# A routed two-layer kernel: eight weight buffers instead of six, loads asked for six tiles ahead instead of four, and other places for one phase's side steps

## The reference

```
x = x + 0.5 * ffn(layernorm(x))      # top 3 of 12 experts, hidden 512
x = x + attn(layernorm(x))           # gated linear recurrence over a sequence, norm, gated matmuls
x = x + 0.5 * ffn(layernorm(x))      # same weights as the first

# ffn: topw, sel = top_k(x @ Wg, 3); softmax over topw
# h = gelu(x @ Wup[e] + bup[e]);  y = h @ Wdown[e] + bdown[e];  sum over the 3 chosen, weighted
```

## Time and profile before

| | |
|---|---|
| median of 3 runs | 636.06 us (634.11 to 636.55) |
| the profiled execution | 638.49 us, span 636.8 us |
| TensorE matmul, weight load | busy 89%, 84% of the span |
| VectorE, ScalarE, GpSimd | busy 55%, 66%, 66% |
| HBM | 96.6 MB read, 30.8 MB written |

### The profile page before, as it was taken

How to read it: one execution, slowest core, us unless ns; L and a number is a source line. 1 busy time by engine, 2 the same in 40 slices (tenths; PEclk the granted TensorE clock), 3 DMA queues, 4 the chain that set the end, 5 groups by cost and what they waited for, 6 DMA issues and landing times.

```text
span 636.8 us, 17884 instructions
## 1 busy us (share of the span) xinstructions
PE 567.4 (89%) x4591; PEld 532.4 (84%) x4591; DVE 349.0 (55%) x1636; ACT 418.8 (66%) x1280; POOL 418.3 (66%) x432
## 2 busy tenths in 40 slices
PE   8469999999899999999989889999998999999505
PEld 7359999999799889979889878889988999999502
DVE  5973365472114688977717568887762632232206
ACT  2546686686466797888657578977766866666204
POOL 1147777777777774556677777046667777777774
PEclk9768999999899999999999899999999999999857
DMA  7676777789598776566488867365659798775137
GB/s 215 178 197 171 216 209 200 220 211 270 157 284 255 218 231 174 139 187 185 132 250 222 268 171 224 105 194 182 181 162 271 210 285 245 216 216 174 48 117 243
DMA packets 121846, 127.90 MB, mean 201 GB/s; under 512 B 17177, under 2 KB 84560, under 8 KB 121748
## 3 DMA queue, kind: packets, MB, share of 16 engines
q1 hardware_dynamic: 106452, 99.52, 52.6%
q0 software_dynamic: 12992, 26.11, 14.8%
q10 hardware_dynamic: 2304, 1.11, 0.6%
HBM read 96.62 MB, written 30.79 MB: 200 GB/s over the span
## 4 chain that ended last, share of the span: by engine, by line
PE 49%; POOL 15%; DMA 12%; issue 10%; DVE 8%; SPq 5%; ACT 1%; DVEq 0%; POOLq 0%; ACTq 0%
PE ps L930 18%; PE ps L943 17%; POOL YG L738 7%; POOL xs L722 4%; DMA xl<-xn,SG 4%; PE ps L798 3%; POOL yk L749 2%; SPq L562 2%; PE ps L900 2%; DMA xs<-XN,SX 2%; DMA yk<-Ys,row 2%; PE ps L824 2%; DMA WU<-in_L_ffn_Wup_dram 2%; POOL xl L707 2%; DMA YG<-ys,SY 2%
## 5 line engine op out<-in xcount | busy, mean ns | idle before, releaser
L1096 ACT ACTIVATE hT<-ps,BU 128x128 f32<-128x128 f32 x944 | 268.6, 371 | 120.4 <-PE ps L930 116.7
L930 PE MATMUL ps<-xT,WU 128*128 128x128 f32 x1888 | 256.2, 279 | 12.8 <-DMA WU<-in_L_ffn_Wup_dram 8.7
L943 PE MATMUL ps<-WD,hT 128*128 x1888 | 252.9, 278 | 2.7 <-DVE Ys L1634 1.8
L930 PEld LDWEIGHTS ps<-xT,WU 128*128 128x128 f32 x1888 | 234.7, 195 | 23.5 <-issue 13.4
L943 PEld LDWEIGHTS ps<-WD,hT 128*128 128x128 f32 x1888 | 232.8, 194 | 4.2 <-issue 4.2
L722 POOL DMA_INDIRECT xs<-XN,SX x144 | 144.3, 1002 | 95.1 <-issue 74.0
L738 POOL DMA_INDIRECT YG<-ys,SY x144 | 150.5, 1045 | 45.2 <-issue 41.8
L1634 DVE TENSOR_TENSOR Ys<-ps,BD 128x128 f32<-128x128 f32 x236 | 67.7, 289 | 204.0 <-PE ps L943 198.1
L707 POOL DMA_INDIRECT xl<-xn,SG x59 | 60.1, 1018 | 31.0 <-issue 13.1
L749 POOL DMA_INDIRECT yk<-Ys,row x59 | 58.8, 996 | 18.0 <-issue 11.6
L1073 ACT ACTIVATE xT<-ps 128x512 f32<-128x512 f32 (+1 forms) x55 | 32.6, 593 | 7.1 <-PE ps L900 3.3
(11 more groups left out here) (255 smaller groups left out, 539.1 us busy)
## 6 DMA issues: line engine op xcount, KB each, us to landing
WU<-in_L_ffn_Wup_dram SPq DMA_DIRECT2D x236, 256.0 KB
ys<-Ys SPq DMA_DIRECT2D x42, 256.0 KB
xl<-xs SPq DMA_DIRECT2D x118, 66.0 KB, 1.9
xl<-xs SPq DMA_DIRECT2D x59, 64.0 KB, 2.0
WD<-in_L_ffn_Wdown_dram SPq DMA_DIRECT2D x12, 256.0 KB, 5.1
WD<-yk SPq DMA_DIRECT2D x4, 768.0 KB, 7.2
xs<-XN,SX POOLq DMA_INDIRECT x144
YG<-ys,SY POOLq DMA_INDIRECT x144
```

What stands on the lines that cost most here:

```text
L930: x = e.matmul(HB[i % 2][:, c * P:(c + 1) * P], WU[i % NW][:, c * P:(c + 1) * P], xT[m % 2][:, j * P:(j + 1) * P], start=True, stop=True)
L943: x = e.matmul(YB[i % 2][:, 0:D], hT[i % 3][:, c * P:(c + 1) * P], WDf[:, bass.ds(r + c * P, P)], start=(c == 0), stop=(c == C - 1))
L1096: x = e.activation(hT[i % 3][:, c * P:(c + 1) * P], HB[i % 2][:, c * P:(c + 1) * P], ACT.Gelu, bias=BU[:, bass.ds(b + c, 1)])
```

## The change

`NW` goes from 6 to 8. At tile `i` SP asks for the weights of tile `i + 6`; at the very first tile for those of 4, 5 and 6. And the last four numbers of each entry of `CHAIN`, the places in the third phase, are others; those of the second phase, the tables and the fourth phase's lists stay.

```
-NW = 6
+NW = 8
...
-    ("V", "G0", (10, 17, 25, 30, 10, 17, 24, 30)),
-    ("V", "G2", (14, 20, 27, 34, 14, 20, 26, 32)),
-    ("V", "S1", (15, 21, 28, 36, 15, 20, 27, 33)),
-    ("A", "G", (17, 23, 29, 38, 17, 22, 28, 35)),
-    ("PA", "A1", (18, 24, 31, 39, 18, 23, 30, 36)),
-    ("PA", "A2", (18, 25, 34, 40, 18, 24, 33, 39)),
-    ("V", "C1", (18, 26, 35, 42, 18, 25, 33, 40)),
-    ("AV", "C2", (19, 27, 37, 42, 19, 25, 35, 41)),
-    ("V", "C3", (23, 28, 38, 43, 21, 26, 35, 41)),
-    ("P", "A3", (24, 30, 39, 44, 23, 28, 37, 43)),
-    ("V", "S3", (24, 30, 39, 45, 23, 28, 37, 43)),
-    ("V", "S3'", (24, 31, 39, 46, 23, 29, 37, 44)),
-    ("A", "A3", (25, 33, 40, 47, 24, 30, 39, 45)),
-    ("PA", "A4", (27, 34, 41, 49, 25, 32, 40, 46)),
-    ("PA", "A5", (28, 35, 42, 50, 26, 34, 42, 48)),
-    ("V", "U5", (29, 36, 43, 51, 27, 34, 43, 48)),
-    ("PV", "A7", (31, 38, 44, 52, 28, 36, 44, 50)),
-    ("PA", "T", (32, 39, 45, 53, 30, 38, 45, 51)),
-    ("V", "N", (32, 39, 44, 52, 30, 39, 45, 50)),
-    ("V", "N'", (33, 41, 44, 53, 32, 40, 45, 50)),
-    ("PV", "L", (33, 40, 47, 53, 32, 39, 46, 52)),
-    ("A", "N", (35, 42, 46, 54, 33, 41, 47, 53)),
-    ("PVG", "K", (35, 41, 49, 55, 35, 41, 48, 54)),
+    ("V", "G0", (10, 17, 25, 30, 10, 17, 22, 29)),
+    ("V", "G2", (14, 20, 27, 34, 12, 19, 25, 30)),
+    ("V", "S1", (15, 21, 28, 36, 14, 19, 25, 30)),
+    ("A", "G", (17, 23, 29, 38, 15, 20, 27, 33)),
+    ("PA", "A1", (18, 24, 31, 39, 19, 22, 29, 34)),
+    ("PA", "A2", (18, 25, 34, 40, 20, 23, 31, 37)),
+    ("V", "C1", (18, 26, 35, 42, 20, 24, 31, 37)),
+    ("AV", "C2", (19, 27, 37, 42, 21, 25, 32, 38)),
+    ("V", "C3", (23, 28, 38, 43, 21, 27, 32, 38)),
+    ("P", "A3", (24, 30, 39, 44, 23, 28, 34, 40)),
+    ("V", "S3", (24, 30, 39, 45, 23, 28, 34, 40)),
+    ("V", "S3'", (24, 31, 39, 46, 23, 28, 34, 41)),
+    ("A", "A3", (25, 33, 40, 47, 24, 30, 36, 43)),
+    ("PA", "A4", (27, 34, 41, 49, 25, 31, 38, 44)),
+    ("PA", "A5", (28, 35, 42, 50, 26, 33, 39, 45)),
+    ("V", "U5", (29, 36, 43, 51, 26, 33, 39, 45)),
+    ("PV", "A7", (31, 38, 44, 52, 28, 35, 40, 47)),
+    ("PA", "T", (32, 39, 45, 53, 29, 36, 41, 48)),
+    ("V", "N", (32, 39, 44, 52, 32, 36, 42, 48)),
+    ("V", "N'", (33, 41, 44, 53, 35, 37, 45, 48)),
+    ("PV", "L", (33, 40, 47, 53, 36, 40, 46, 49)),
+    ("A", "N", (35, 42, 46, 54, 36, 40, 46, 49)),
+    ("PVG", "K", (35, 41, 49, 55, 37, 41, 47, 52)),
...
-                if i + 4 < NI:
-                    load_w(i + 4)
+                for x in (4, 5, 6) if i == 0 else (i + 6,):
+                    if x < NI:
+                        load_w(x)
```

## The result

The changed kernel takes 638.17 us in the median of 20 runs (635.5 to 641.38), beside 635.38 us for 20 runs of the kernel before. The ratio is 1.0034, 95% interval 1.0018 to 1.0049: slower by 2.2 us by that ratio and by 2.8 us between the medians, within the 0.5% that the prediction called no change, and not 4.2 us faster. Its profiled execution took 640.42 us, 2.3 us above the median.

A forecast was written before the change was run, and what follows sets the result against it. The prediction took GpSimd's unbroken chain of indirect DMAs as the bound. The fourth phase's first gather was to start at 484.4 instead of 488.6 us, so 4.2 us off the 636.06 us median gives 631.8 us, range 627 to 638.5.

The forecast's parts named there:

- What bounds the kernel: GpSimd's unbroken chain of 119 indirect DMAs from 473.16 us; the last quarter's scatter start plus 155.4 and 8.2 us sets the end.
- The weight waits: TensorE's waits at third-phase tiles 4 and 16, with the lower clock behind them, worth 4.7 + 2.7 = 7.4 us.
- Part 1 alone: Eight buffers and loads six tiles ahead, by themselves, advance TensorE in the third phase by 8.3 us.
- The closing up: GpSimd's 48 third-phase scatters run without idle stretches and end at 484.2 us, not 488.3.
- K of quarter 0: Third phase: VectorE waits for gathers until 364.9 us, the step ends at 421.6, its first scatter starts at 422.4, not 420.18.
- The failed step: SP at the last border: the fourth phase's first rows, queued behind loads and a store, cost 0 to 1 us, taken 0.
- level: The third phase's last outputs land at about 484.3 us, as the fourth phase's first gather, at 484.4, needs them.
- (e): Rival: TensorE's K must wait for L on VectorE, phase ends 5 us later, 638 to 641 us; chance 0.10.
- (a): Rival: gathers don't bind, TensorE sets K; first K scatter at 417.8, 8 to 9 us saved, 627.5 us; chance 0.15.
- (d): Rival: weights come no earlier since DMA engines are full; first K scatter at 427.6, 637 us; chance 0.05.
- (b): Rival: VectorE and TensorE, both full, lose 3 to 6 us more; only former idle stretches won, 634 to 637 us; chance 0.25.
- (c): Rival: VectorE scans and GpSimd gathers collide twice as often at shared ports, 3 us more, 634.8 us; chance 0.05.

The follow-up runs named there:

- before_again: The kernel before, unchanged, run and profiled a second time: 635.93 us, ratio 0.9991.
- buffers_only: The kernel before with eight weight buffers and loads six tiles ahead, old places kept: 633.85 us, ratio 0.9976 to the kernel before.
- after_third: The changed kernel once more, no load held back: 638.44 us, ratio 1.0035 to the kernel before.
- old_held_last_2: The changed kernel with the old places and the loads held back at the last phase border alone: 631.58 us in 6 runs, ratio 0.9914 to the kernel before.
- held_at_border: The changed kernel with loads six tiles ahead inside a phase but in the old order across each phase border: 634.01 us, ratio 0.9962 to the kernel before.
- old_places_held: The changed kernel with the old places and loads held back at all three phase borders: 633.15 us, ratio 0.9969 to the kernel before.
- held_last: The changed kernel, new places, with loads held back at the last phase border alone: 634.40 us, ratio 0.9977 to the kernel before.
- old_held_last_2 and 3: Two runs of one kernel, the changed one with old places and loads held back at the last border alone: 631.58 and 631.29 us.
- places_only: The changed kernel with six weight buffers and loads four tiles ahead, new places kept: 635.05 us, ratio 0.9991 to the kernel before.

## Why the prediction was wrong

**What bounds the kernel: right.** From the first gather of the fourth phase to the end of the execution it is 149.7 to 150.7 us in the sixteen profiles. The time is decided, within 1 us, by when that gather starts.

**The weight waits: gone, but their price was that of one execution.** The earlier trace rows priced tiles 4 and 16 at 4.7 us of waits and 2.7 us of lower clock. In before_again the waits are 2.06 and 1.50 us, and the clock did not fall behind either. Tile 24 starts at 378.48 and not 381.68, and everything to the end is 3.1 us earlier. So 3.1 of the 4.2 us forecast were in the profile's execution (638.49 us) and not in the median (635.4 to 635.9), from which I took the whole 4.2. Against that second execution the step should have read: first gather 484.4 against 485.5, 1 us. Part 1 alone was to put TensorE 8.3 us ahead; K0 of buffers_only is 5.9 us earlier than in the first profile and 2.7 us earlier than in the second.

**The closing up: right. K of quarter 0: right in the number, in part by luck.** The first scatter was forecast at 422.4 and came at 424.16 and 421.42, VectorE waited for gathers at the steps of tiles 12 and 19 (and 17), and no idle stretch is left. Without the wait for outputs the first gather could have started at 486.5 and 483.7, around the forecast 484.4. But two terms of the sum were off and cancelled. VectorE was to go on at tile 19 at 364.9, 2.3 us after the 24th gather's start. It went on at 368.85 and 366.02, 5.3 and 4.5 us after that start (363.56, 361.52), and 4.1 to 4.9 us after it in the six other profiles with all the new places; the DMA engines were full there (DMA share 1.02, 324 GB/s from 360 to 369 us). From there to the end of K it was to be 56.7 us and was 54.5 and 54.6. That K0 comes 2.7 us later in the first profile than in the second has 1.8 us of its cause in a later start of the third phase (321.45, 319.69), and 1.0 us at tile 23, where TensorE waits 3.04 us for a `bias_down` and not 2.05.

**The failed step** is the one on SP: "They wait for 36 scatters anyway: cost 0 to 1 us, taken 0", and with it "level" for the last outputs. I asked when the rows would be issued, and that was right (473.47, 473.33 before). I did not ask what would lie in the DMA queue in front of them. Four loads behind one table wait put the use of the rows some 1 us back, TensorE's idle time there was 2.1 to 3.3 us and not 0 to 1.0, its granted clock was 0.57 to 0.61 over the 4 us behind it, and the stores that hang behind the first tiles' gelus held up the first gather for 2.8 to 4.2 us after the scatters had ended.

The last outputs were to be in memory at 484.3; the gather that waits for them started at 490.64 and 486.44. That 484.3 rested on 486.03 as the landing of all of them, and the row does not say which store landed then: the last one had gone out at 482.20, and in the five profiles the gather starts 4.8 to 6.2 us after it goes out. Nor was there slack to spend: the closing up that the prediction itself forecast brings the scatters' end 2.1 to 2.6 us nearer to the issue of the rows. Against a usual execution the sum, made after the fact, is then -1 + 3 to 4 = 2 to 3 us; 2.2 us are measured by the ratios and 2.6 to 2.8 between the medians.

The Trainium skill, DMA: Bandwidth & Descriptors, section Two DMAs through the same engine are not ordered, says that within one queue of one DMA engine descriptors start in order, though they need not finish writing in order, and that nothing orders transfers across the 16 engines. By that rule the rows' descriptors on each engine would start behind those of the weights. The traces fit it (3.3 to 4.2 us from issue to use in the five profiles with four loads in front, 2.0 to 3.1 in the eleven with two), but rows that merely shared the bandwidth with the loads (DMA share 1.06, 364 GB/s from 472 to 476 us) would look the same; no run here separates the two.

**The rivals.** None names this mechanism. (e) gives the time, 638 to 641, but not by its condition: K0 of the changed kernel never came later than 424.2. (a) and (d) fall by K0 (and (a)'s 8 to 9 us could not have been had in any case: the last outputs, forecast at 484.3, leave at most 4.3), (b) by the closed-up scatters. (c), the ports, shows no trace: the 48 gathers of the third phase took 50.7 us in all before and 50.1 after (50.1 and 49.4 in the second profiles).

**What the places are worth: nothing that shows.** In after_third TensorE starts tile 35 2.25 us later than in old_held_last_2 (409.74, 407.49), behind its two waits for `bias_down`, and K stands two tiles on (6.7 us). Less the 1.3 us by which K follows its tile more closely, K0 is 7.7 us later. The closing up returns 6.2 of them: 53.0 us from K0 to the last quarter become 46.8. Net 1.5 us lost in this pair of profiles; the medians say 0.9 us (held_at_border, old_places_held, which is within the noise) to 3 us (held_last, old_held_last_2 and 3, which is not). In places_only, against the kernel before, they come to 0.9991 (0.997 to 1.0011), nothing. I compared the places with a kernel that had the weight waits; I should have compared them with the one that the first part makes.

## What to carry to other kernels

A load asked for earlier is earlier in its queue as well: at every point where a deeper prefetch crosses a wait, list what now goes out in one burst behind that wait and in front of what. Take the base of a sum from an execution near the median, or scale it to one; a stall with a clock fall behind it may be in one execution and not in the next. Cost the parts of a change against each other's result, not each against the old kernel: here the first part with four lines for the border gave 0.3 to 0.9% (2 to 5.6 us; old_places_held, old_held_last_2 and 3), and the second gave nothing on top and may have taken up to 4 us away. A step that closes one queue up also shortens the time that others had beside it.

## What was not expected of the hardware

TensorE idled 2.04 us ahead of tile 4 in the first profile before, and the next `up` and `down` took 1.37 and 1.92 us. It idled 2.06 us at the same place in the second, and they took 1.16 and 1.06; the granted clock from 332 to 336 us was 0.62 in the first and 1.00 in the second. The length of an idle stretch alone does not decide whether the clock falls:

```profile
330.63 1.16 PE L930 MATMUL ps<-xT,WU 128*128 128x128 f32 x8 [2.06 <-DMA WU<-in_L_ffn_Wup_dram]
331.62 1.06 PE L943 MATMUL ps<-WD,hT 128*128 x8
```
